# Storing the feed-forward activations in interleaved pairs of tiles, and quantising them in two steps of four

## The reference, cut to what matters

```python
h = bit_linear(x, w1)                     # 256 -> 1024; x quantised per token to 8 bits, w1 to -1, 0, 1
h = depthwise_conv1d(h.transpose(0, 2, 1), conv_w, conv_b)   # 3 taps along the tokens, per channel
h = h.transpose(0, 2, 1)
h = silu(h)
return bit_linear(h, w2)                  # 1024 -> 256; h quantised per token

def act_quant(x):                         # inside bit_linear
    scale = 127.0 / clip(max(abs(x), axis=-1, keepdims=True), 1e-05)
    return clip(round(x * scale), -128, 127) / scale
```

## Time and profile before

| | |
|---|---|
| median of 3 runs | 1667.87 us (1667.2 to 1668.99) |
| the profiled execution's own time | 1667.05 us |
| its span, first to last instruction | 1665.0 us |
| TensorE busy | 1473.7 us, 89% |
| VectorE busy | 1278.9 us, 77% |
| ScalarE busy | 1181.7 us, 71% |
| GpSimd busy | 728.5 us, 44% |

### The profile page before, as it was taken

How to read it: one execution, slowest core, us unless ns; L and a number is a source line. 1 busy time by engine, 2 the same in 40 slices (tenths; PEclk the granted TensorE clock), 3 DMA queues, 4 the chain that set the end, 5 groups by cost and what they waited for, 6 DMA issues and landing times.

```text
span 1665.0 us, 33467 instructions
## 1 busy us (share of the span) xinstructions
PE 1473.7 (89%) x10778; PEld 1189.6 (71%) x10778; DVE 1278.9 (77%) x3029; ACT 1181.7 (71%) x3925; POOL 728.5 (44%) x1085
## 2 busy tenths in 40 slices
PE   7999999989899999989899998989999898988642
PEld 3678777777777777777777777777777777777521
DVE  4263787888878798787878888887878878787876
ACT  2477877858687786968778686867778596877621
POOL 0144445445544445544444544454444445444400
PEclk9999999999999999999999999999999999999855
DMA  7300001000000101000010100000010000000000
GB/s 188 118 28 24 19 15 42 15 27 13 26 28 13 40 13 40 1 26 28 14 39 13 40 13 25 15 26 27 13 40 13 27 13 26 28 1 27 0 13 13
DMA packets 41129, 47.14 MB, mean 28 GB/s; under 512 B 3008, under 2 KB 35200, under 8 KB 41088
## 3 DMA queue, kind: packets, MB, share of 16 engines
q1 hardware_dynamic: 40032, 45.82, 8.9%
q10 hardware_dynamic: 1056, 0.81, 0.2%
HBM read 36.13 MB, written 10.49 MB: 28 GB/s over the span
## 4 chain that ended last, share of the span: by engine, by line
PE 40%; DVE 28%; ACT 20%; issue 11%; DMA 0%; POOL 0%; DVEq 0%; ACTq 0%; POOLq 0%
ACT SM L648 7%; DVE GBS L877 7%; PE PS L460 7%; PE PS L422 6%; PE PS L438 4%; PE PS L521 4%; PE PS L447 4%; PE PS L403 4%; PE PS L473 3%; PE PS L412 3%; DVE GBS L888 2%; ACT H L673 2%; ACT GBS L678 2%; DVE GBS L867 2%; DVE H L895 2%
## 5 line engine op out<-in xcount | busy, mean ns | idle before, releaser
L1030 POOL TENSOR_TENSOR SM<-SM,RC 128x496 f32<-128x496 f32 (+1 forms) x512 | 339.8, 685 | 710.8 <-DVE RC L802 710.8
L648 ACT ACTIVATE SM<-PS,MX 128x124 f32<-128x124 f32 x1024 | 358.8, 365 | 195.7 <-DVE SM L808 193.6
L460 PE MATMUL PS<-KT,QM 128*128 128x128 f32 x2048 | 277.9, 279 | 21.9 <-ACT SM L648 21.8
L460 PEld LDWEIGHTS PS<-KT,QM 128*128 128x128 f32 x2048 | 249.4, 192 | 34.9 <-ACT SM L648 33.7
L1062 POOL TENSOR_TENSOR OTl<-OF,OTh 128x256 fp32r<-128x256 f32 x256 | 216.0, 844 | 5.6 <-ACT OF L642 5.6
L648 ACT ACTIVATION_READ_ACCUMULATOR SM<-PS,MX 128x1 f32 x1024 | 212.3, 207 | 0.0
L447 PE MATMUL PS<-IDF,SM 128*128 128x128 f32 x1024 | 169.0, 288 | 18.8 <-POOL SM L1030 18.7
L640 ACT ACTIVATE OTh<-PS 128x256 fp32r<-128x256 f32 x256 | 99.4, 388 | 108.6 <-PE PS L438 104.7
L806 DVE TENSOR_REDUCE MX<-PS 128x4 f32<-128x496 f32 x256 | 170.2, 665 | 0.0
L438 PE MATMUL PS<-PT,V 128*64 128x128 f32 x2048 | 169.7, 287 | 0.0
L438 PEld LDWEIGHTS PS<-PT,V 128*64 128x64 f32 x2048 | 107.5, 137 | 82.4 <-issue 75.9
(11 more groups left out here) (140 smaller groups left out, 3691.2 us busy)
## 6 DMA issues: line engine op xcount, KB each, us to landing
XIN<-in_x SPq DMA_DIRECT2D x16, 512.0 KB, 3.5
XRES<-in_x SPq DMA_DIRECT2D x16, 512.0 KB, 3.5
out_y<-H SPq DMA_DIRECT2D x16, 512.0 KB, 3.0
CRAW<-in_ctxT SPq DMA_DIRECT2D x16, 256.0 KB, 2.7
RRAW<-in_ctxT SPq DMA_DIRECT2D x32, 128.0 KB, 2.8
QM<-in_Wq SPq DMA_DIRECT2D x1, 1024.0 KB, 10.8
GBS<-in_Wo SPq DMA_DIRECT2D x1, 1024.0 KB, 22.1
k_ipa_columns<-H SPq DMA_DIRECT2D x1, 1024.0 KB, 6.0
```

The source lines that it names most:

```text
L460: m = mm(psS[:, h, :], QM[:, 2 * q + h // 2, h % 2, TOK * b:TOK * b + TOK], KT[:, 2 * q + h // 2, b, :], start=True, stop=True)
L648: m = act.activation(SM[s % 2][:, h, 0:ORG], psS[:, h, 0:ORG], ACT.Exp, bias=MX[s % 2][:, h:h + 1], accum_out=SU[s % 2][:, h:h + 1])
L1030: m = pool.tensor_tensor(part, part, RC[c % 2][:, 4 * i:4 * i + 4].unsqueeze(2).broadcast_to(shape), ALU.mult)
```

## The change

The activations are stored as four pairs of tiles, `HP = [P, CT // 2, T, 2]`. Within a pair the values of the even and of the odd tile alternate, so value t of tile j stands next to value t of its partner, and consecutive values of one tile are two floats (8 bytes) apart. All instructions that read or write an activation tile (lines 673, 678, 852, 858, 872, 888 and 1042) now go over every second float. The four maxima of line 877 walk, for each token, over four places 1024 floats apart with two adjacent floats at each. The rounded tiles, the first quantisation's data and the output rows keep their contiguous places in the same memory ("h_rows"), so a rounded tile now overwrites part of a pair, and both tiles of that pair must have been multiplied first.

The second quantisation is done in two half steps of four tiles (n = 33 and 34) instead of three of three, three and two. DVE multiplies three tiles and then rounds four; POOL multiplies tiles 3 and 7. DVE still has six of the eight multiplications. POOL's multiplication of tile 7 waits until tile 3 has been rounded. The waits of the rounding are placed so that a pair is only overwritten after both its tiles were read.

```diff
-Q2_DVE = CT - CT // 3
+Q2_DVE = CT - CT // 4
...
-        H = sb("H", [P, CT, T])
+        HP = sb("HP", [P, CT // 2, T, 2])
...
-        XN2 = H[:, 6:8, :].rearrange("p a (b d) -> p (a b) d", d=DM)
-        Q1 = H[:, 5, :].bitcast(BF16).rearrange("p (b d) -> p b d", d=DM)
-        Q2 = [H[:, j, 0:T // 2].bitcast(BF16) for j in range(CT)]
-        OUTT = H[:, 0:NB, T // 2:T]
+        HT = [HP[:, j // 2, :, j % 2] for j in range(CT)]
+        h_flat = HP[:].rearrange("p k t i -> p (k t i)")
+        h_rows = h_flat.rearrange("p (j t) -> p j t", j=CT)
+        XN2 = h_rows[:, 6:8, :].rearrange("p a (b d) -> p (a b) d", d=DM)
+        Q1 = h_rows[:, 5, :].bitcast(BF16).rearrange("p (b d) -> p b d", d=DM)
+        Q2 = [h_rows[:, j, 0:T // 2].bitcast(BF16) for j in range(CT)]
+        OUTT = h_rows[:, 0:NB, T // 2:T]
...
-                    act.activation(H[:, j, :].rearrange("p (b t) -> p b t", b=NB), GB[j % 4], ACT.Identity,
+                    act.activation(HT[j].rearrange("p (b t) -> p b t", b=NB), GB[j % 4], ACT.Identity,
...
-                        dve.tensor_reduce(HM[:, b, :], H[:, :, TOK * b:TOK * b + TOK].rearrange("p j t -> p t j"), AX.X, ALU.max,
+                        dve.tensor_reduce(HM[:, b, :], HP[:, :, TOK * b:TOK * b + TOK, :].rearrange("p k t i -> p t k i"), AX.XY, ALU.max,
                                           apply_absolute_value=True).then_inc(hm_done, 1)
...
-                    if n == M_Q2 + j // 3 and j % 3 < 2:
+                    if n == M_Q2 + j // 4 and j % 4 < 3:
                         dve.wait_ge(bc_done, g.count(2, 2))
                         if j >= 4:
                             dve.wait_ge(q2_done, g.count(CT, j - 3))
-                        dve.tensor_tensor(GB[j % 4].rearrange("p b t -> p (b t)"), H[:, j, :], BC[:], ALU.mult).then_inc(q2_scaled[0], 1)
+                        dve.tensor_tensor(GB[j % 4].rearrange("p b t -> p (b t)"), HT[j], BC[:], ALU.mult).then_inc(q2_scaled[0], 1)
                 for j in range(CT):
-                    if n == M_Q2 + j // 3:
-                        if j % 3 < 2:
-                            dve.wait_ge(q2_scaled[0], g.count(Q2_DVE, j - j // 3 + 1))
-                        else:
-                            dve.wait_ge(q2_scaled[1], g.count(CT - Q2_DVE, j // 3 + 1))
+                    if n == M_Q2 + j // 4:
+                        if j % 4 == 0:
+                            dve.wait_ge(q2_scaled[0], g.count(Q2_DVE, 3 * (j // 4) + 2))
+                        if j % 4 == 2:
+                            dve.wait_ge(q2_scaled[0], g.count(Q2_DVE, 3 * (j // 4) + 3))
+                            dve.wait_ge(q2_scaled[1], g.count(CT - Q2_DVE, j // 4 + 1))
                         dve.tensor_scalar(Q2[j], GB[j % 4].rearrange("p b t -> p (b t)"), MAGIC, MAGIC,
                                           ALU.add, ALU.subtract).then_inc(q2_done, 1)
...
-                    if n == M_Q2 + j // 3 and j % 3 == 2:
+                    if n == M_Q2 + j // 4 and j % 4 == 3:
                         pool.wait_ge(bc_done, g.count(2, 2))
                         if j >= 4:
                             pool.wait_ge(q2_done, g.count(CT, j - 3))
-                        pool.tensor_tensor(GB[j % 4].rearrange("p b t -> p (b t)"), H[:, j, :], BC[:], ALU.mult).then_inc(q2_scaled[1], 1)
+                        pool.tensor_tensor(GB[j % 4].rearrange("p b t -> p (b t)"), HT[j], BC[:], ALU.mult).then_inc(q2_scaled[1], 1)
```

More of the change, by code:

```diff
@@ L275, in program @@
         cir_t = SM[1][:].rearrange("p a t -> p (a t)")[:, 0:256]
-        h_flat = H[:].rearrange("p a t -> p (a t)")
         ki_all = h_flat[:, 0:2048].rearrange("p (g k n) -> p g k n", g=GROUPS, k=PAIRS)
@@ L677, in finish @@
                     act.wait_ge(t3_done, g.count(CT, j + 1))
-                    act.activation(GB[j % 4], H[:, j, :].rearrange("p (b t) -> p b t", b=NB), ACT.Tanh,
+                    act.activation(GB[j % 4], HT[j].rearrange("p (b t) -> p b t", b=NB), ACT.Tanh,
                                    scale=0.5).then_inc(th_done, 1)
@@ L850, in finish @@
                     dve.wait_ge(t2_done, g.count(CT, j + 1))
-                    y = H[:, j, :].rearrange("p (b t) -> p b t", b=NB)
+                    y = HT[j].rearrange("p (b t) -> p b t", b=NB)
                     dve.scalar_tensor_tensor(out=y[:, :, 0:TOK - 1], in0=GB[j % 4][:, :, 1:TOK], scalar=CW[:, j, 2:3],
```

## The result

| | before | changed |
|---|---|---|
| median | 1668.43 us (1667.2 to 1670.17, 4 runs) | 1634.16 us (1631.61 to 1634.99, 4 runs) |
| profiled execution, its span | 1667.05, 1665.0 us | 1633.91, 1631.8 us |

The ratio is 0.9782, with a 95% interval of 0.977 to 0.9794. The forecast was 1641.6 us; 34 us were gained where it had 26.

A forecast was written before the change was run, and what follows sets the result against it. No owner on the chain; each 94.9 us group is PE's work plus about 7.3 us standing still. Maxima gain 37.5 us, strided passes nothing, two steps cost 11.2: 26.3 us gained, 1641.6 us, range 1630 to 1660.

The forecast's parts named there:

- The maxima: Line 877's four reductions fall from 1922 to 1220 ns each, which gains 37.5 us in all.
- rival (b): At line 877 each jump costs as before, 1571 ns, while 8-byte steps are free: 1656.6 us; chance 0.10.
- (d): Line 877's new walk is no faster, 1922 ns, leaving only the two steps' 11.2 us: 1679 us; chance 0.05.
- its whole idle time and no more: At line 505 PE gains just its wait for the maxima, 2.31 us a group, with 0.65 us to spare.
- fifteen times 2.31: PE's waits at line 505 in all groups but the last, taken as equal: 34.7 us gained.
- The strided passes: Passes over single tiles in 8-byte steps on ACT, DVE and POOL cost nothing; upper bound 0.18 us a pass.
- the 10 ns I allowed: Medians of lines 673, 678, 858, 852, 872 and 888 were to stay within 10 ns of before.
- The second quantisation: Two steps make PE 0.8 us later in each of 14 groups, 11.2 us; bounds nothing and 1.4 us.
- the 0.46 us wait: PE's wait at line 521 for the last rounding disappears, absorbing 0.46 of the 1.3 us delay at line 447.
- The sum: Whole kernel: 37.5 us for the maxima less 11.2 for the two steps, 26.3 us gained, 1641.6 us.
- (c): Strided passes of lines 673, 678, 872 and 888 pay 0.18 us each, 34 us: about 1690 us; chance 0.09.

The follow-up runs named there:

- slow_walk: layout_only with only the maxima's reading order changed: four even tiles of a token first, then the four odd; 1669.57 us, ratio 0.9996 to the kernel before.
- layout_only: The kernel before with the interleaved pairs but the old three steps, rounded tiles and output rows in other free places; 1618.47 us, ratio 0.9689.
- the prices: The changed kernel with 31 instructions appended after its last transfer, run one at a time at various steps and distances; each price measured once, adjacent-pair reductions 1.22 us.
- pool_none: The changed kernel with all eight multiplications of the second quantisation on DVE, none on POOL; 1610.16 us, ratio 0.9648 to the kernel before.
- pool_one_tile: The changed kernel with tile 7 multiplied by DVE too, so POOL has tile 3 only; 1632.16 us, ratio 0.9777 to the kernel before.
- pool_behind: The changed kernel with POOL's multiplication of tile 7 put behind its attention step instead of ahead of it; 1658.16 us, ratio 0.9932 to the kernel before.
- two_steps_only: The kernel before, on its old contiguous tiles, with the second quantisation in two steps of four; 1699.04 us, ratio 1.0184.

## Why the forecast came out as it did

The direction and the mechanism of the maxima were right; 8 us of the gain were missed, in terms of both signs. The experiments give a ladder of full-clock periods: 94.9 before, 95.3 with the layout and the old walk (slow_walk), 92.5 with the new walk (layout_only), 93.0 with the two steps too. In these the half clock stretches number 7, 3, 0 and 6 of 13.

- **The maxima.** Forecast 1220 ns, measured 1208. That excludes the 1571 ns of rival (b) and the 1922 of (d), and the prices show why: pairs cost 1.22 us, as adjacent values do. Of the gain on PE's path, "its whole idle time and no more", 2.31 us a group, the step from slow_walk to layout_only shows 2.8 at full clock. The idle time itself is 2.2 of it. The rest can be read off PE's starts in the two kernels:

```profile
907.96 0.39 PE L476 MATMUL PS<-WOh,OTl 128*128 128x256 f32 x2
908.46 0.50 PE L415 MATMUL PS<-CTh,WKh 128*128 128x512 f32 x1
...
909.50 0.40 PE L415 MATMUL PS<-CTR,WKRl 128*128 128x512 f32 x1
912.13 0.66 PE L508 MATMUL PS<-IDF,GBS 128*128 128x128 f32 x4 [2.23 <-DVE GBS L880]
```

```profile
889.26 0.39 PE L476 MATMUL PS<-WOh,OTl 128*128 128x256 f32 x2
889.49 0.40 PE L415 MATMUL PS<-CTh,WKh 128*128 128x512 f32 x1
...
890.43 0.39 PE L415 MATMUL PS<-CTR,WKRl 128*128 128x512 f32 x1
890.66 0.60 PE L508 MATMUL PS<-IDF,GBS 128*128 128x128 f32 x4
```

From the start of the last product of line 415 to line 508 it is 2.63 us in slow_walk and 0.23 in layout_only, 2.40 apart: products overlap by 0.17 us when they follow one another, and a wait costs that too. At the first product of line 415, between the two pairs of maxima, another 0.27 us go (0.50 against 0.23). Also, the waits of the earlier trace rows are not fifteen times 2.31: fourteen are 2.2 us, the fifteenth, that of the last group but one, is 3.86.
- **The strided passes.** Forecast nothing. DVE: nothing. ACT: 46 ns a pass, outside the 10 ns I allowed. From before to slow_walk the period grew by 0.36 us, which holds these and the moved output rows. 0.25 us of it is idle time of PE at line 463, waiting for ACT, 1.3 us a group before and 1.5 after, and 0.1 is at line 415; that ACT's longer passes are the cause fits, but was not tried alone. DVE's medians did not stay within 10 ns as forecast: line 890's went from 694 to 1207 ns, and is 688 in pool_none, where POOL has no tile.
- **The second quantisation.** Forecast 0.8 us a group, measured 0.5 at full clock (layout_only to the changed kernel). The fourth rounding was due at 827.15 - 822.2 = 4.95 us after BC and came at 4.9. POOL's queue moved as described, and PE's wait grew by 1.14 us where I had 1.3. PE took in more of it than the 0.46 us wait: from line 449's start to line 523's it now needs 820.10 - 816.83 = 3.27 us against 832.90 - 828.94 = 3.96, 0.69 less. But pool_one_tile shows that POOL's tile was not the only thing that was late, and pool_none that without POOL's tiles the two steps cost nothing at full clock (92.0 us against 92.0).
- **The step that failed** is that of the price of a stall, "it gains its whole idle time and no more". A stall costs some 0.2 us more than its idle time at full clock, as above, and a stall of 2.1 to 2.2 us also has, in some periods, some three microseconds at half clock behind it, worth 1.3 to 1.6 us. The sum left that out on both sides. With it the two steps cost 16 us on the new layout (0.5 us x 14 + 6 stretches x 1.5 = 16) and 30 on the old, where I had 11.2; it is also part of why the walk was worth 51 us where I had 37.5. In the change as a whole seven stretches went (9.5 us) and six came (9.3 us), so in the steady part the miss cancelled, and that was luck: nothing in the sum foresaw it. 25.6 us were gained in 13 periods against a forecast of 13 x 1.51 = 19.6. Most of the 6 us between come from the terms above: 13 times 0.5 us more for the maxima and 0.3 less for the two steps, less 0.36 for the passes.
- **The tail.** Behind the 13 periods 7.1 us were gained, where one more wait and the last group's maxima, less one second quantisation, had 4.3. The fifteenth wait fell from 3.86 to 1.12 us and the last from 12.5 to 10.0. Ahead of the 13 periods only 0.5 us of the first group's 2.3 show: PE's first line 449 came at 89.6 us where line 447 had come at 87.7, for a reason that was not found. 1.7 us of the 7.1 is clock again, the last product of the last group, at the lower level before and at the upper after:

```profile
1657.10 3.59 PE L521 MATMUL PS<-W,H 128*128 128x256 bf16 x16 [0.97 <-DVE H L818]
```

```profile
1625.62 1.92 PE L523 MATMUL PS<-W,HP 128*128 128x256 bf16 x16 [0.97 <-DVE HP L820]
```

The Trainium skill ("Advanced Engine Details and Errata", section SBUF Cachelines) asks for two hits on a 16-byte line. The prices agree: 1.22 us with two fp32 values to a line, 1.95 with one, and 1.50 at steps of 12 bytes, where one line in three gives two.

The chances of the prediction do not quite add up by direction: (c) and (d) alone have 0.14, and slower was given 0.13.

## What to carry to other kernels

Interleave tiles two by two when one instruction has to walk across them: the walk then runs at the speed of adjacent values, and passes over single tiles stay in 8-byte steps, which DVE does for nothing and ACT for 0.03 to 0.05 us each; four by four overshoots. Before pricing a stall of the matrix engine at its idle time, look at several periods with the granted clock beside them; if they come in two lengths, removing or adding a stall of two microseconds can be worth more than it lasts. And a change made of two parts deserves to be timed as two: here one part gave 50 us and the other took 16 back.

## What the hardware showed that I had not expected

- The half clock of TensorE appears at or behind single waits of 1.8 to 2.2 us. It was never seen in the steady part of the three kernels whose longest wait was 1.0 to 1.2 us, and not each long wait brings it: 7 of 13 periods before, 3 in slow_walk and 6 in the changed kernel with 2.1 to 2.2 us, 5 in pool_one_tile with 1.9, 2 in pool_none with 2.1, and 12 in pool_behind with 1.84 and a second wait close behind. In two_steps_only it came at line 505 in all 13 periods, behind the same 2.2 us that brought it in 7 before. So the length of the wait alone does not decide. What does was not found.
- A reduction reads at 12-byte steps in 1.50 us, between 1.22 at 8 and 1.95 at 16. ACT pays 0.03 us for 8-byte steps alone, in the running kernel 0.046.
- Beyond 16 bytes distance is nearly free: 1.95, 1.98, 1.87 and 1.93 us at 16, 32, 2048 and 2064 bytes.
